# A decoder layer whose engines test 81 lines of semaphore waits less, in the same order of work

## The reference

```
x = x + attn(layernorm(x))            # 16 heads of 8, rope, causal, softmax
x = x + xattn(layernorm(x), ctx)      # 16 heads of 8 against the 77 context rows
x = x + ffn(layernorm(x))             # shared expert + 2.0 * top1 value * one of 7 routed experts
```

## Time and profile before

| | us |
|---|---|
| median of 3 runs (1092.92 to 1093.52) | 1093.27 |
| the profiled execution's own time | 1091.68 |
| its span from first to last instruction | 1089.3 |
| PE busy | 1007.5 (92%) |
| PEld busy | 859.1 (79%) |
| DVE busy | 852.5 (78%) |
| ACT busy | 744.4 (68%) |
| POOL busy | 628.8 (58%) |
| chain that ended last: PE | 64% |
| the same: issue of the four row DMAs (L391) | 11% |
| the same: landing of those DMAs | 10% |

### The profile page before, as it was taken

One profiled execution on the slowest core, in us unless ns is written; L12 is line 12 of the kernel. 1 busy time (PEld: TensorE's weight loads), 2 busy tenths in 40 slices (PEclk: granted clock), 3 DMA queues, 4 the chain that ended last, 5 costly groups with the idle time before them and its releaser, 6 DMA issues.

```text
span 1089.3 us, 49897 instructions
## 1 busy us (share of the span) xinstructions
PE 1007.5 (92%) x16232; PEld 859.1 (79%) x16233; DVE 852.5 (78%) x2853; ACT 744.4 (68%) x1557; POOL 628.8 (58%) x1488
## 2 busy tenths in 40 slices
PE   2689999999999999999999999999998879999995
PEld 1567788778877788777877788777877879999995
DVE  3357889888888888888888888888885557777774
ACT  0367887888878887888878888888864235555552
POOL 0345767667667766677667766776654214444443
PEclk9899999999999999999999999999999989999998
DMA  5222110001000100001000100011100122222220
GB/s 130 66 70 71 28 37 26 26 28 33 25 25 25 35 26 25 25 29 32 25 25 25 36 25 25 25 31 32 28 23 20 49 76 70 74 71 65 70 69 5
DMA packets 66661, 44.41 MB, mean 41 GB/s; under 512 B 24135, under 2 KB 61451, under 8 KB 66592
## 3 DMA queue, kind: packets, MB, share of 16 engines
q1 hardware_dynamic: 55424, 30.35, 10.3%
q0 software_dynamic: 5312, 12.18, 3.3%
q10 hardware_dynamic: 5856, 0.99, 0.6%
HBM read 23.96 MB, written 18.29 MB: 39 GB/s over the span
## 4 chain that ended last, share of the span: by engine, by line
PE 64%; SPq 12%; DMA 11%; issue 3%; ACT 2%; DVE 2%; POOL 1%; ACTq 0%; DVEq 0%; POOLq 0%
SPq L391 11%; DMA arena<-arena 10%; PE pv L1198 6%; PE scores L1383 6%; PE scores L1388 6%; PE ro L1400 6%; PE scores L1247 5%; PE scores L1240 5%; PE ro L1255 4%; PE scores L1110 4%; PE ro L1207 4%; PE pj L1307 3%; PE scores L1102 3%; PE st L1311 2%; ACT arena L913 2%
## 5 line engine op out<-in xcount | busy, mean ns | idle before, releaser
L991 ACT ACTIVATE arena<-scores 128x1024 f32<-128x1024 f32 (+1 forms) x256 | 260.6, 1019 | 56.5 <-PE scores L1110 36.2
L668 DVE TENSOR_REDUCE arena<-scores 128x8 f16<-128x1024 f32 (+1 forms) x256 | 255.1, 997 | 35.8 <-PE scores L1084 25.6
L913 ACT ACTIVATE arena<-st 128x128 f16<-128x128 f16 (+2 forms) x256 | 155.2, 606 | 22.0 <-PE st L1311 7.7
L1198 PE MATMUL pv<-arena 128*32 128x128 f32 (+1 forms) x4096 | 139.2, 277 | 0.3 <-issue 0.3
L913 ACT ACTIVATE arena<-arena 128x512 f16<-128x512 f32 (+2 forms) x192 | 93.0, 485 | 45.7 <-DVE arena L717 40.0
L448 POOL TENSOR_TENSOR arena<-arena,neg_half 128x1 f32<-128x1 f32 x192 | 106.4, 554 | 29.1 <-POOL arena L439 10.9
L1198 PEld LDWEIGHTS pv<-arena 128*32 128x32 f32 (+1 forms) x4096 | 104.7, 110 | 13.9 <-issue 1.1
L549 POOL DMA_INDIRECT out_dram<-x_tile x70 | 69.4, 992 | 38.4 <-POOL carried L548 26.1
L518 POOL DMA_INDIRECT xs<-pay,put x64 | 69.3, 1083 | 27.3 <-issue 27.3
L867 DVE SCALAR_TENSOR_TENSOR half_hid<-tanh_s,scores 128x512 f32<-128x512 f32 x70 | 48.1, 687 | 40.9 <-ACT tanh_s L1040 40.9
L1311 PE MATMUL st<-id,arena 128*128 128x128 f16 (+1 forms) x1024 | 73.9, 215 | 4.7 <-POOL arena L477 4.3
(11 more groups left out here) (175 smaller groups left out, 2658.1 us busy)
## 6 DMA issues: line engine op xcount, KB each, us to landing
x_tile<-xs SPq DMA_DIRECT2D x70, 129.0 KB, 2.1
arena<-arena SPq DMA_DIRECT2D x512, 4.0 KB
arena<-in_x_dram SPq DMA_DIRECT2D x64, 64.0 KB
out_dram<-pay SPq DMA_DIRECT2D x64, 64.0 KB, 1.6
arena<-in_ctx_dram SPq DMA_DIRECT2D x64, 38.5 KB
w_gate<-in_L_ffn_gate_w_dram SPq DMA_DIRECT2D x7, 256.0 KB, 2.8
w_up<-in_L_ffn_up_w_dram SPq DMA_DIRECT2D x7, 256.0 KB, 3.1
w_down<-in_L_ffn_down_w_dram SPq DMA_DIRECT2D x7, 256.0 KB, 3.7
```

The costliest lines, as they stand in the source:

```text
L668: v.tensor_reduce(nmax[:, n, :].rearrange("p (m r s) -> p r m s", r=2, s=SLOT)[:, u, :, 0:HG], pair(s)[:, :, 0:HG * keys].rearrange("p m ( ...
L913: return a.activation(to, of, ACT.Copy)
L991: a.activation(e32[0:rows, 2 * n + u, :], scores[0:rows, 1024 * s:1024 * (s + 1)], ACT.Exp).then_inc(sexp_done[n][u], 1)
L1198: last = t.matmul(pv[SLOT * j:SLOT * (j + 1), 0:2 * P].rearrange("p (c a y) -> p a c y", a=2, y=SLOT)[:, a], vals[0:rows, p, at0:at0 + SLO ...
```

## The change

Two kinds of tests are taken out, and nothing is moved. (1) 81 lines `wait(...)` whose condition another wait of the same engine, earlier in its order or beside it, already implies. (2) The call of `turn` for ten TensorE pieces gets an empty list of users: `project_out` 0, `xT_of` 1, `stacks`, the second `cross_for_max`, `project_kv2`, the first pair of interleaved score pieces (two lists), `values` 1, `stacks2`, `router`. The order of the instructions that compute, all semaphore increments, all tiles and all DMAs are as before.

```diff
@@ SyncE
             def load_ctx(b, p):
-                wait(sync, ctxT_psum, b - 1)
                 sync.dma_start(ctx_t[0:C, p, :], ctx_in[b]).then_inc(ctx_in_s[p], 16)
@@ GpSimd
                 wait(pool, ln_mv[n], b + 1)
-                wait(pool, ln_rstd[n], b)
                 if n == 2:
-                    wait(pool, ln3_shift, b)
                     g.tensor_tensor(neg_mean[:, :], mv[:, 2, p, 0:1], neg_one[:, :], ALU.mult)
                 g.tensor_tensor(varp[:, n:n + 1], mv[:, n, p, 1:2], eps[:, :], ALU.add).then_inc(ln_var[n], 1)
-                if n == 0:
-                    wait(pool, rot_ready, b - 1)
-                    wait(pool, val_ready, b - 1)
-                elif n == 1:
-                    wait(pool, q2_ready, b - 1)
-                else:
-                    wait(pool, xn3_ready, b - 1)
                 wait(pool, ln_var[n], b + 1)
...
@@ VectorE (of some 30 lines)
             def add_attention(b, p):
                 wait(dve, proj_psum[0], b + 1)
-                wait(dve, xb_ready[0], b + 1)
-                wait(dve, xb_ready[1], b - 1)
-                wait(dve, ln_stats[1], b - 1)
-                wait(dve, xT_psum[1], b - 1)
...
@@ ScalarE
             def nmT_copy(b, p, n):
                 wait(act, nmT_psum[n], b + 1)
-                wait(act, max_rows[n][p], 32 * b - 32 * p)
                 copy(nmaxT[:, n, p, :], st16[:, 0:P]).then_inc(nmT_ready[n], 1)
...
             def k2_high(b, p):
                 wait(act, k2_ready, b + 1)
-                wait(act, qkT2_psum, b - 1)
...
@@ TensorE
-            def cross_for_max(b, p, u, s, now, *before):
+            def cross_for_max(b, p, u, s, *users):
-                wait(pe, qkT2_ready, b + 1)
-                turn(pe, b, now, *before)
+                turn(pe, b, *users)
...
-            def values(b, p, n, now, *before):
+            def values(b, p, n, *users):
                 vals, rows = ((val, P), (val2, C))[n]
-                wait(pe, sexp_done[n][0], b + 1)
                 wait(pe, sexp_done[n][1], b + 1)
-                wait(pe, (val_ready, val2_ready)[n], b + 1)
...
             def positions(b, p, *users):
                 wait(pe, hot_ready, b + 1)
-                wait(pe, run_ready, b)
...
@@ TensorE's step (tuples of the calls cut)
-                at(i, p, 8, project_out, 0, ((resid_done[1], -2),), ...
+                at(i, p, 8, project_out, 0)
-                at(i, p, 6, stacks, ((nmT_ready[0], 0),), ...
+                at(i, p, 6, stacks)
-                at(i, p, 8, project_kv2, ((ctxT_ready, 1),), ...
+                at(i, p, 8, project_kv2)
...
@@ tile phase
-                wait(dve, t_up, k - 1)
-                    wait(dve, ty_psum, k - 2)
-                wait(act, t_gate, k - 1)
-                    wait(act, t_half, k - 2)
-                    wait(act, t_up, k - 1)
-                    wait(pe, t_mul, k - 2)
-                    wait(pe, tT_ready, k)
```

More of the change, by code:

```diff
@@ L498, in add_out_bias @@
             def add_out_bias(b, p, n):
-                if n:
-                    wait(pool, resid_done[0], b + 1)
-                else:
+                if n == 0:
                     wait(pool, x_in_s[p], 8 * b + 16 - 8 * p)
@@ L950, in values2_in @@
             def values2_in(b, p):
-                wait(act, k2_ready, b + 1)
                 wait(act, pv_done[1], b - 1)
@@ L1113, in cross_exp_round, with self_for_max @@
                     last.then_inc(sexp_psum[1][u], 1)
-            def self_for_max(b, p, u, s, now, *before):
+            def self_for_max(b, p, u, s, *users):
                 wait(pe, qkT_ready, b + 1)
-                turn(pe, b, now, *before)
+                turn(pe, b, *users)
                 for h in range(4):
@@ L1122, in self_for_max, with self_for_exp @@
                     self_max_round(s, u, p, g)
-            def self_for_exp(b, p, u, s, now, *before):
+            def self_for_exp(b, p, u, s, *users):
                 wait(pe, max_rows[0][p], 32 * b + 64 - 32 * p)
-                turn(pe, b, now, *before)
+                turn(pe, b, *users)
                 for h in range(4):
@@ L1131, in self_for_exp, with cross_for_exp @@
                     self_exp_round(s, u, p, g)
-            def cross_for_max(b, p, u, s, now, *before):
-                wait(pe, qkT2_ready, b + 1)
-                turn(pe, b, now, *before)
+            def cross_for_max(b, p, u, s, *users):
+                turn(pe, b, *users)
                 for g in range(HG):
                     cross_max_round(s, u, p, g)
-            def cross_for_exp(b, p, u, s, now, *before):
+            def cross_for_exp(b, p, u, s, *users):
                 wait(pe, max_rows[1][p], 32 * b + 64 - 32 * p)
-                turn(pe, b, now, *before)
+                turn(pe, b, *users)
                 for g in range(HG):
@@ L1202, in values, with project_out, xT_of @@
                 last.then_inc(pv_done[n], 1)
-            def project_out(b, p, n, now, *before):
+            def project_out(b, p, n, *users):
                 wait(pe, oT_ready[n], b + 1)
-                turn(pe, b, now, *before)
+                turn(pe, b, *users)
                 t.matmul(ro[:, 0:P], oT[:, n, :], (w_o, wc_o)[n][:, :], start=True, stop=True).then_inc(proj_psum[n], 1)
-            def xT_of(b, p, n, now, *before):
+            def xT_of(b, p, n, *users):
                 if n == 0:
@@ L1244, in shared_up @@
             def shared_up(b, p, s):
-                wait(pe, xT_ready[2], b + 1)
                 for c in range(FC):
@@ L1249, in shared_up, with shared_down @@
                 last.then_inc(sh_up, 1)
-            def shared_down(b, p, now, *before):
+            def shared_down(b, p, *users):
                 wait(pe, sh_hid, b + 1)
-                turn(pe, b, now, *before)
+                turn(pe, b, *users)
                 for c in range(FC):
@@ L1285, in busy_pj, with positions @@
                     t.matmul(pj[:, c * P:(c + 1) * P], w_qkv[:, 0:P], w_qkv[:, 0:P], start=True, stop=True)
-            def positions(b, p, now, *before):
+            def positions(b, p, *users):
                 wait(pe, hot_ready, b + 1)
-                wait(pe, run_ready, b)
-                turn(pe, b, now, *before)
+                turn(pe, b, *users)
                 cols = ro[:, 2 * P:2 * P + 2 * E].rearrange("p (n e) -> p n e", n=2)
@@ L1297, in positions, with ctxT_of, project_kv2 @@
                 last.then_inc(pos_psum, 1)
-            def ctxT_of(b, p, now, *before):
+            def ctxT_of(b, p, *users):
                 wait(pe, ctx_in_s[p], 8 * b + 16 - 8 * p)
-                turn(pe, b, now, *before)
+                turn(pe, b, *users)
                 t.transpose(pj[:, 3 * D:3 * D + C], ctx_t[0:C, p, :], id32[0:C, 0:C]).then_inc(ctxT_psum, 1)
-            def project_kv2(b, p, now, *before):
+            def project_kv2(b, p, *users):
                 wait(pe, ctxT_ready, b + 1)
-                turn(pe, b, now, *before)
+                turn(pe, b, *users)
                 t.matmul(pj[0:C, 0:2 * D], ctxT[:, 0:C], wc_kv[:, :], start=True, stop=True).then_inc(kv2_psum, 1)
@@ L1313, in stack4, with stacks, stacks2, nmT_of @@
                 return last
-            def stacks(b, p, now, *before):
+            def stacks(b, p, *users):
                 wait(pe, qk_lo, b + 1)
-                turn(pe, b, now, *before)
+                turn(pe, b, *users)
                 stack4(0, parts[:, p, HD:], P, P)
                 stack4(4 * P, parts[:, p, H * SLOT:], P, P).then_inc(qkT_psum, 1)
-            def stacks2(b, p, now, *before):
+            def stacks2(b, p, *users):
                 wait(pe, q2_lo, b + 1)
-                wait(pe, k2_lo, b + 1)
-                turn(pe, b, now, *before)
+                turn(pe, b, *users)
                 stack4(0, parts_q2[:, p, :], P, P)
                 stack4(4 * P, parts_k2[:, p, :], C, CP).then_inc(qkT2_psum, 1)
-            def nmT_of(b, p, n, now, *before):
+            def nmT_of(b, p, n, *users):
                 wait(pe, smax_done[n][0], b + 1)
                 wait(pe, smax_done[n][1], b + 1)
-                turn(pe, b, now, *before)
+                turn(pe, b, *users)
                 t.transpose(st16[:, 0:P], nmax[:, n, :], id16[:, :]).then_inc(nmT_psum[n], 1)
```

98 lines of the change are left out of this document (21 added, 77 removed).

## The result

The kernel after takes 1085.25 us (median of 4 executions, 1085.04 to 1086.83), the kernel before 1093.1 in the same comparison (1092.17 to 1093.52): a ratio of 0.9933, 95% interval 0.9915 to 0.995. It is faster, by 7.9 us where 13 were forecast. The profiled execution after was the slowest of its four, 1086.83 (span 1084.9).

The account below looks back on a forecast made before the run. TensorE's chain in the attention phase was taken as the bound, VectorE nearly as late. 24 plain steps gave 4.3 us, 24 with the branch 8.4, 15 unrolled 1.2, together 13.9: 1079.4, rounded to 1080; range 1070 to 1092.

Parts of the forecast that it names:

- What bounds the kernel: Attention phase: TensorE's chain sets the time, VectorE nearly as late; savings count only as far as VectorE's results allow.
- (a): ScalarE's copy of the row maxima: a register operation leaves the chain, 0.08 us in each of 48 loop steps.
- (b): TensorE's transpositions, stacks, positions: 0.10 us per plain step, 0.15 with the branch, 0.08 unrolled; hot_of is the bound.
- The four pieces: Sign: TensorE's two transposition pieces, stacks and positions, each reaching its best, sum to about 0.83 us.
- (c): Step with the branch: GpSimd's scaled comes earlier, so turned_back and all behind it do; 0.12 us for 24 steps.
- (d): All other removals, including nearly all of VectorE's, SyncE's one and the tile phase: nothing, since their tests are covered.
- The unrolled steps: 15 steps outside the loop, 0.08 us each from the last of TensorE's pieces, 0.28 towards 0.18; together 1.2 us.
- the slower rival: Context load issued sooner meets the row DMAs, landing 2.73 instead of 1.77 us; 1118 if 40 steps hit; chance 0.06.
- the sequencer piece in front of the copy: Sign: no sequencer piece remains on the chain between TensorE's transposition of the maxima and ScalarE's copy.
- L1207's second piece: Sign: in the step with the branch, this piece between xT_of and shared_up is near 0.22 us, from 0.34.
- the round: Sign: a loop round takes about 23.9 us instead of 24.46; above 24.3, another engine binds.
- The small gain: Rival: VectorE's chain and ScalarE's copies keep their pace, only (a) is left, 3.8 us, time 1089.5; chance 0.19.

Follow-up runs that it names:

- a1: Kernel before with only ScalarE's wait for max_rows ahead of nmT_copy removed; 2.8 us faster by the medians, the round falls by 0.078.
- a3: Kernel after with TensorE's waits and bank waits all put back, leaving the other four engines' part; 1083.59 us, round 24.313.
- c3: Kernel after with all of VectorE's waits put back; round 24.239 us.
- a2: Kernel before with TensorE's part of the change alone, its waits and ten bank waits; 1089.25 us.
- two edits: Kernel after with marks_of moved behind turned_back(0) and the wait for xb_ready[1] put back in add_cross; 1080.74 us, round 24.135.
- b6: Kernel after with marks_of as a tensor_scalar comparison with one SBUF tensor input instead of two, in its old place; round 24.296 us.

## Why the prediction was right and wrong

The time fell inside the range and on the side that had the chance of 0.82. The forecast of 1080 was 5 us too fast, and its size is right in part by luck: of the 12.7 us that were put into the loop, 3.8 came. The rest of the 7.9 lies outside the loop, where 1.2 were forecast, and some of it in landings of row DMAs that the sum did not have.

- **What bounds the kernel: right.** A saving counted only as far as VectorE's results let TensorE use it. The prediction wrote this sentence, gave it a rival, and did not price it in its sum: VectorE bound in both kinds of step.
- **(a): right in place and size.** 0.08 at the copy in each step, and the first half of the step 0.10 and 0.08 shorter. Taken out alone (a1), half of it came back as waiting for VectorE. ScalarE's own copy before it (`k2_high`), to which the prediction gave about 0.1, now ends at 485.36, and the copy starts at 485.38: nothing is left there.
- **(b): the waiter was wrong, and with it the size.** Not `hot_of` but ScalarE's copy out of bank `ro` is what `positions` waits for. The four pieces in the branch step are 0.11 + 0.07 + 0.45 + 0.31 = 0.94 after, not 0.83: the first three reached their best, and the last took back what they gained. From the last matmul of `shared_up` to the last of `positions` the medians went from 1.129 to 1.083 in the branch step and from 1.086 to 1.083 in the plain one, 0.05 and 0.00 where 0.15 and 0.10 were taken. In a1 and a3, which keep all of TensorE's waits, it is 1.08 in both steps too, so that even the 0.05 isn't the price of these waits alone. The unrolled step, whose sum was 0.09 + 0.45 + 0.28 with its 0.28 unexplained, had shown this: a piece that grows when those before it shrink is waiting.
- **(c): the cause was right, the result not.** GpSimd's `scaled` did come 0.12 earlier against `marks_of`. But `turned_back` was bound by VectorE's own order as well, and the earlier `scaled` stretched `marks_of` there: the second piece of `project_out` is 0.36 instead of the 0.22 forecast (0.34 before).
- **(d): right for the tile phase and, by c3, for VectorE's waits but one.** The one was put at nothing, and its removal cost about 0.08 in the plain step; the prediction allowed no loss here.
- **The unrolled steps** were put at 1.2 us; behind the last branch 3.0 went (2.3 in the second profile of the kernel after), 1.1 of it in the two landings. The landing moved against the slower rival, which had it grow. That `load_ctx` or another wait is its cause wasn't tried; with TensorE's part alone (a2) the two landings are 2.52 and 2.13, with the other engines' part alone (a3) 2.32 and 1.78.
- **Its own signs.** Of those named for the forecast, three came: the sequencer piece in front of the copy is gone, over six waits a step are gone under L328 ((1524 - 735) / 64 = 12), and the tile is unchanged. Three did not: the four pieces sum to 0.94, not 0.83, L1207's second piece is 0.36, not 0.22, and the round is 24.304, not 23.9. It stays above the 24.3 that was the sign of another engine binding, which is what the experiments then showed.
- **The rivals.** The small gain had the right mechanism, VectorE keeping its pace, with 1089.5; the measured time lies between it and the forecast. The loop alone gave the 3.8 us that this rival had for (a), though (a) by itself (a1) kept only 1.9 of them. The sum was off by its terms (b) and (c), 8.9 us for the loop, where the second half of the step measured no change in the mean. Each was priced without what stood right behind it: ScalarE's copy for (b), VectorE's own order for (c).

Still open: of the round's 0.148 in a3, the copy's wait gives 0.078. The rest lies in the second half of the branch step (7.63 in a1, 7.53 in a3); which other waits of the four engines give it was not separated.

## What to carry to other kernels

Taking out an implied wait is worth something only where its engine isn't just about to wait for another, and it can cost, as in `add_cross`. Look, for each piece on the chain, at what it would wait for if it came 0.1 us earlier, and price that. When an engine is made earlier, check which of its operations then runs beside which of its neighbour's. And a removal is worth measuring again after the next bound has gone: TensorE's was worth 0.01 a round here, and 0.195 two edits later, and those two edits were worth nothing while TensorE's waits were in.

## What the runs showed of the hardware

- VectorE's 8-column comparison took 0.18 us alone, 0.22 in its old place, and up to 0.47 (a1) beside a GpSimd operation of 0.41, ending with it; with one SBUF input (b6, up to 0.46) just as with two.
- Taking out a wait made the next instruction later: with the single wait that needs a register, `add_cross` began 0.16 after that sequencer piece had ended (480.08 to 480.24); with an already true wait in front of it, it began 0.05 after. It did so in the loop's plain step only; why, and why not in the other step, stays open.
- A register operation for a wait's count stood for 0.08 us on ScalarE in front of the copy; the wait itself, in the unrolled steps, for nothing that shows (0.256 from transposition to copy there, with it and without).
